# Context key and value projection moved beside the second norm, and the group steps laid out anew

## What is computed

```python
x = x + attn(layernorm(x))                        # causal, 16 heads of 32
h = ln(layernorm(x))                              # two norms in a row
q, k, v, qx = (round_fp8(h / s_i) * s_i @ w_i.T for each of the four)  # 8 groups, 2 heads of 128 each
kx, vx = split(ctx @ w_kv_x.T)                    # 8 groups of 128, no rounding
q, k, qx, kx = (ln of every head's 128 values)
core = softmax(q @ k.T / sqrt(128)) @ v           # 512 keys
xout = softmax(qx @ kx.T / sqrt(128)) @ vx        # 1024 keys
x = x + round_fp8(concat(core, xout) / smooth) @ wproj.T * scale
x = x + top-p mixture of 8 experts (layernorm(x))
```

## Time and profile before

| | |
|---|---|
| median of three runs | 2743.81 us (2742.49 to 2744.0) |
| the profiled execution: time, span | 2739.35 us, 2736.8 us |
| TensorE busy | 2386.2 us, 87% of the span |
| VectorE busy | 1414.3 us, 52% |
| ScalarE busy | 1133.5 us, 41% |
| GpSimd busy | 1044.1 us, 38% |
| first norm and causal attention | 0 to 306 us |
| second norm | 306 to 361 us |
| group attention: up to its first maximum | 361 to 407 us |
| its 16 steps, with the drain | 407 to about 1750 us |
| experts | to the end, TensorE full |

### The profile page before, as it was taken

How to read it: one execution, slowest core, us unless ns; L and a number is a source line. 1 busy time by engine, 2 the same in 40 slices (tenths; PEclk the granted TensorE clock), 3 DMA queues, 4 the chain that set the end, 5 groups by cost and what they waited for, 6 DMA issues and landing times. The chain is left out here.

```text
span 2736.8 us, 43666 instructions
## 1 busy us (share of the span) xinstructions
PE 2386.2 (87%) x15296; PEld 1424.9 (52%) x15296; DVE 1414.3 (52%) x3100; ACT 1133.5 (41%) x2101; POOL 1044.1 (38%) x1219
## 2 busy tenths in 40 slices
PE   6999457888888888788888876799999999999999
PEld 4666245566555566556566543344444444444444
DVE  5666747676676676667676666522222132322221
ACT  4555536565665555566566653211111112111110
POOL 3421235555564463635555341322131313122231
PEclk9898669899999999999999989799999999999999
DMA  3100005464554544555464454401011010112000
GB/s 130 45 21 1 1 1 110 81 120 90 98 107 81 100 99 91 109 97 93 83 116 92 83 103 83 185 32 62 31 61 61 31 61 31 61 34 88 0 0 31
DMA packets 414120, 191.69 MB, mean 70 GB/s; under 512 B 403568, under 2 KB 404080, under 8 KB 407280
## 3 DMA queue, kind: packets, MB, share of 16 engines
q1 hardware_dynamic: 410768, 166.29, 27.5%
q10 hardware_dynamic: 3168, 23.07, 2.6%
HBM read 86.56 MB, written 2.10 MB: 32 GB/s over the span
## 5 line engine op out<-in xcount | busy, mean ns | idle before, releaser
L1602 ACT ACTIVATE sil<-bank 128x512 f32<-128x512 f32 x128 | 76.4, 597 | 772.5 <-PE bank L289 772.5
L1293 DVE TENSOR_REDUCE xnm<-bank 128x1 f32<-128x512 f32 (+1 forms) x256 | 244.9, 957 | 263.7 <-PE bank L289 263.7
L1575 POOL TENSOR_SCALAR hh<-h 128x512 f16<-128x512 f32 x128 | 104.8, 819 | 680.7 <-DVE h L1673 680.7
L1673 DVE TENSOR_TENSOR h<-bank,sil 128x512 f32<-128x512 f32 x128 | 88.5, 692 | 530.7 <-PE bank L289 423.2
L1304 DVE SCALAR_TENSOR_TENSOR xparts<-xprob,xri,xparts 128x512 f16<-128x512 f32 (+1 forms) x256 | 271.2, 1060 | 105.5 <-ACT xparts L1210 103.7
L1210 ACT ACTIVATE xparts<-xprob,xri 128x512 f16<-128x512 f32 (+1 forms) x256 | 240.9, 941 | 204.6 <-DVE xri L1299 150.0
L1202 ACT ACTIVATE xprob<-bank,xnm 128x512 f32<-128x512 f32 (+1 forms) x256 | 231.3, 903 | 134.4 <-DVE xnm L1293 132.5
L287 PE MATMUL bank<-eXTh,ewh_gate 128*128 128x512 f16 x512 | 194.7, 380 | 3.5 <-DVE ewl_gate L1620 3.5
L288 PE MATMUL bank<-eXTh,ewl_gate 128*128 128x512 f16 x512 | 194.6, 380 | 0.0
L289 PE MATMUL bank<-eXTl,ewh_gate 128*128 128x512 f16 x512 | 194.6, 380 | 0.0
L287 PE MATMUL bank<-eXTh,ewh_up 128*128 128x512 f16 x512 | 194.1, 379 | 0.4 <-DVE ewl_up L1620 0.4
(11 more groups left out here) (247 smaller groups left out, 6242.1 us busy)
## 6 DMA issues: line engine op xcount, KB each, us to landing
xwraw<-in_w_group ACTq DMA_DIRECT2D x22, 1024.0 KB, 5.5
raw_gate<-in_gate SPq DMA_DIRECT2D x8, 2048.0 KB, 7.6
raw_up<-in_up SPq DMA_DIRECT2D x8, 2048.0 KB, 8.0
raw_down<-in_down SPq DMA_DIRECT2D x8, 2048.0 KB, 7.8
craw<-in_ctx SPq DMA_DIRECT2D x4, 1024.0 KB, 7.5
xpt<-xparts SPq DMA_TRANSPOSE x256, 4.3
wraw<-in_w_qkv SPq DMA_DIRECT2D x4, 768.0 KB, 4.4
X<-in_x SPq DMA_DIRECT2D x8, 256.0 KB, 5.0
```

The costliest lines, as they stand in the source:

```text
L1293: dve.tensor_reduce(nm[:, s:s + 1], SC[u % 2][:, 0:L], AX.X, ALU.max, negate=True).then_inc(maxed, 1)
L1575: pool.tensor_scalar(hh[half][:, f, :], h[i % 2][:], 1.0, 1.0, ALU.mult, ALU.mult).then_inc(h_hi, 1)
L1602: act.activation(sil[i % 2][:], bank[:, 2 * (i % 2), :], ACT.Silu, scale=1.0 / WS).then_inc(silu, 1)
L1673: dve.tensor_tensor(h[i % 2][:], bank[:, 2 * (i % 2) + 1, :], sil[i % 2][:], ALU.mult).then_inc(made, 1)
```

## The change

The projection of context keys and values leaves the group steps. `second_norm` now runs it for all groups: 4 pairs of groups by 2 batch entries by 8 context tiles, 64 tiles, each 12 matmuls of 512 columns into one of four PSUM banks, with the key norm (16 blocks at a time, the shifts half on GpSimd and half on VectorE), the key turns, and the high and low parts; the result goes to a DRAM tensor `kv_d`. The norm's own turns and roundings are placed between the tiles. The first pair's weights are split in the causal stage. Behind the phase all semaphores so far are cleared and freed, and a barrier follows. A group step loads keys and values of its batch entry from `kv_d` (a DMA of 1024 KB each, issued by ScalarE).

The steps are laid out anew: no C, T5 and T6 jobs; A and B one per unit in units 0 to 5, Y in 8 to 11, T in 12 to 15; product lag 6 instead of 4; 8 slots for turned parts instead of 4; 4 buffers for the parts instead of 2; q parts for both batch entries; GpSimd applies all 20 shifts; the weights of k and v in a chunk and a buffer of their own; the order of the instructions within a unit is another on VectorE and on ScalarE.

```diff
@@ -85,41 +85,54 @@
     out_d = out.rearrange("b (t p) d -> (b t) p d", p=P)
...
         with ExitStack() as ctx:
             rows2 = norm_rows(sem, lambda n, s, d: sbuf(ctx, n, s, d), "n2")
             rcols = sbuf(ctx, "rcols", [P, COLS], F32)
...
+            gw = [sbuf(ctx, f"x{x}", [P, KT, c], F16)
+                  for x, c in (("w1h", S), ("w1l", S), ("w2h", 2 * DH), ("w2l", 2 * DH))]
+            kv_d = nc.dram_tensor("kv_made", (B, GROUPS, P, KV), F16, kind="Internal").ap()
+            with ExitStack() as cross:
+                cxh, cxl = (sbuf(cross, x, [P, KT, B * SX], F16, "right") for x in ("cxh", "cxl"))
+                kvw = [[sbuf(cross, f"kv{x}{i}", [P, KT, S], F16, "right") for x in ("h", "l")] for i in range(2)]
+                kvraw = sbuf(cross, "kvraw", [P, KT, S], F32, "right")
+                with ExitStack() as c1:
+                    XTh = sbuf(c1, "XTh", [P, KT, T], F16)
...
                 with ExitStack() as c2:
-                    first_norm(nc, ins, sem, lambda n, s, d: sbuf(c2, n, s, d), bank, X, ident, cols, XTh, XTl, x_d, w)
-                with ExitStack() as c2:
-                    causal_attention(nc, ins, sem, lambda n, s, d: sbuf(c2, n, s, d), bank, X, ident, cols, XTh, XTl,
-                                     w, cxh, cxl, gw, rows2)
-            xq = sbuf(ctx, "xq", [P, 4, KT, T], F16)
+                    second_norm(nc, ins, sem, lambda n, s, d: sbuf(c2, n, s, d), bank, X, ident, cols, xq, rcols,
+                                rows2, cxh, cxl, kvw, kvraw, kv_d)
+            clear()
...
+                group_attention(nc, ins, sem, lambda n, s, d: sbuf(c2, n, s, d), bank, X, ident, cols, rcols, xq, kv_d,
+                                gw, rows3)
...
-    gwraw = [sb(f"gwraw{i}", [P, KT, S], F32) for i in range(2)]
+    gwraw = [sb("gwraw0", [P, KT, S], F32), sb("gwraw1", [P, KT, 2 * DH], F32)]
+    early = [(gwraw[0], gw[0], gw[1], group_scales(cols, 1)), (gwraw[1], gw[2], gw[3], group_scales(cols, 2)),
+             (kvraw, kvw[0][0], kvw[0][1], [(k, slice(0, S), WS) for k in range(KT)])]
...
 XT = SX // P
...
-SLOTS = 4
+SLOTS = 8
+PARTS_KEPT = 4
+LAG = 6
 P_SCALE = 2.0 ** 15
 PAIRS = UX // 2
-BLOCKS = KINDS * BT + BT + XT
...
+PAIRS_G = GROUPS // 2
+BATCH = XT
+BATCHES = PAIRS_G * B
...
+TURN_OFFSETS = (5, 6, 7, 7)
...
+def turns_at(i):
+
+    return [(i // BATCH - 1, r) for r, o in enumerate(TURN_OFFSETS) if i >= BATCH and i % BATCH == o]
...
+def norms_at(i):
...
+    j = i - NORM_FROM
+    return [j // NORM_EVERY] if j >= 0 and j % NORM_EVERY == 0 and j // NORM_EVERY < B * KT else []
...
+            for q in range(BATCHES):
+                gp, b = q // B, q % B
+                sp.wait_ge(c_low, BATCH * (q + 1))
+                for g in range(2):
+                    sp.dma_start(kv_d[b, 2 * gp + g, :, 2 * SX:4 * SX], vst[q % 2][:, g, :]).then_inc(v_stored[q % 2], 16)
+                if q in (0, 2):
+                    load(2 + q // 2)
+                for g in range(2):
+                    sp.wait_ge(t_lo, 4 * q + 2 * (g + 1))
+                    sp.dma_start(kv_d[b, 2 * gp + g, :, 0:2 * SX], kst[:, g, :]).then_inc(k_stored[g], 16)
...
+                for t in range(BATCH):
+                    a = kr[q % 2][:, 0, t, :]
+                    pool.tensor_scalar(a, a, rstd[:, t:t + 1], shift[:, t:t + 1], ALU.mult, ALU.add)\
+                        .then_inc(applied_pool, 1)
+                for r in range(4):
+                    k = 4 * q + r
+                    pool.wait_ge(t_read, k + 1)
+                    pool.tensor_tensor(key_part(r, 1), ft[k % 2][:], key_part(r, 0), ALU.subtract).then_inc(t_lo, 1)
+                if q in (1, 3):
+                    weights(2 + q // 2)
...
+                if i in (2, 3):
+                    normalise(1, i - 2)
+                if i == NORM_FROM:
+                    act.wait_ge(s_rcols, 2)
+                for j in norms_at(i - 1):
+                    scaled(j)
+                for q, r in turns_at(i):
+                    read_turned(q, r)
+            for r in range(4):
+                read_turned(BATCHES - 1, r)
...
         def _(dve):
+            def low(i):
+                q, t = i // BATCH, i % BATCH
+                dve.wait_ge(c_read, i + 1)
+                dve.scalar_tensor_tensor(out=value_part(i, 1), in0=cross_bank(i)[:, :, 1, :], scalar=1.0 / WS,
+                                         in1=value_part(i, 0), op0=ALU.mult, op1=ALU.subtract).then_inc(c_low, 1)
+                if q >= 2 and t == 0:
+                    dve.wait_ge(c_shift, q - 1)
+                for g in range(2):
+                    dve.bn_stats(stats[q % 2][:, BATCH * g + t, :], kr[q % 2][:, g, t, :]).then_inc(c_stats, 1)
...
+            for i in range(CROSS):
+                low(i)
+                for j in norms_at(i - 2):
+                    rounding(j)
+                if i >= BATCH and i % BATCH == 4:
+                    apply(i // BATCH - 1)
+                if i in (1, 27, 43):
+                    weights(1 + (1, 27, 43).index(i))
+            apply(BATCHES - 1)
...
+            def project(i):
+                gp, b, t = i // (B * BATCH), i // BATCH % B, i % BATCH
+                tok = slice(SX * b + P * t, SX * b + P * (t + 1))
+                wh, wl = kvw[gp % 2]
+                if i >= 4:
+                    pe.wait_ge(c_low, i - 3)
+                if i % (B * BATCH) == 0 and gp:
+                    pe.wait_ge(kw_lo, KT * gp)
+                for k in range(KT):
+                    ins_ = three(pe, bank[:, 2 + i % 4, :], cxh[:, k, tok], cxl[:, k, tok], wh[:, k, :], wl[:, k, :],
+                                 k == 0, k == KT - 1)
+                ins_.then_inc(c_done, 1)
...
-JOBS = "A0 A1 A2 A3 B0 B1 C0 C1 C2 C3 Y0 Y1 Y2 Y3 T0 T1 T4 T2 T3 T5 T6".split()
-
-SLOT_JOBS = {0: ("A0", "A1"), 1: ("A2", "A3"), 2: ("B0", "B1"), 3: ("C0",), 4: ("C1",), 5: ("C2",), 6: ("C3",),
-             7: ("Y0",), 8: ("Y1",), 9: ("Y2",), 10: ("Y3", "T0"), 11: ("T1", "T4"), 12: ("T2",), 13: ("T3", "T5"),
-             14: ("T6",)}
-APPLY_AT = {9: range(0, 5), 10: range(5, 11), 11: range(11, 4 * BT)}
-POOL_APPLIES = range(4 * BT, BLOCKS)
+            def turn(q, r):
+                k, g, half = 4 * q + r, r // 2, r % 2
+                if g == 0:
+                    pe.wait_ge(applied_pool, BATCH * q + BT * (half + 1))
+                else:
+                    pe.wait_ge(applied_dve, BATCH * q + BT * (half + 1))
+                if k >= 2:
+                    pe.wait_ge(t_read, k - 1)
...
+                ins_.then_inc(t_done, 1)
+
+            for i in range(CROSS):
+                project(i)
+                for j in norms_at(i):
+                    turn_norm(j)
...
+JOBS = "A0 A1 A2 A3 B0 B1 Y0 Y1 Y2 Y3 T4 T0 T1 T2 T3".split()
+
+SLOT_JOBS = {0: ("A0",), 1: ("A1",), 2: ("A2",), 3: ("A3",), 4: ("B0",), 5: ("B1",), 8: ("Y0",), 9: ("Y1",),
+             10: ("Y2",), 11: ("Y3",), 12: ("T4",), 13: ("T0",), 14: ("T1",), 15: ("T2", "T3")}
+APPLY_ORDER = [4 * BT + t for t in range(BT)] + list(range(4 * BT))
+OUTPUT_AT = {10: 0, 14: 1, 2: 2, 6: 3}
+ROUND_AT = {11: 0, 15: 1, 3: 2, 6: 3}
+QUANTISED_AT = {13: (0, 0), 0: (1, 1), 4: (2, 1), 7: (3, 1)}
 NEXT = [j for j in JOBS if j[0] != "Y"]
 T_ORDER = [j for j in JOBS if j[0] == "T"]
-V_ORDER = [j for j in JOBS if j[0] in "BC"]
+V_ORDER = [j for j in JOBS if j[0] == "B"]
 
...
-    return JOBS.index(name) % 2
+    i = JOBS.index(name)
+    return (i if i < 6 else i + 1) % 2
...
+                    if u in QUANTISED_AT and not (first and QUANTISED_AT[u][1]):
+                        kind, late = QUANTISED_AT[u]
+                        quantised(n - late, kind)
+                    if b == 0 and u == 4 and not last_group:
+                        split(1, 2 * g + 1, w_base(g), next_done, next_count("A3", n + 1), 4 * KT * g + 2 * KT)
+                    if b == 1 and u == 0 and not last_group:
+                        split(2, g + 1, w_base(g) + W1N, next_done, next_count("B1", n), 4 * KT * (g + 1))
                     if b == 1 and u == 3:
-                        split(3, 3 * g + 3 if not last_group else 3 * g + 1, w_base(g) + (0 if last_group else W1N + W2N),
+                        split(3, 2 * g + (2 if not last_group else 1), w_base(g) + (0 if last_group else W1N + W2N),
                               y_done, BT * (n - 1))
...
+            def load_kv(g, b, free):
+                wait(pved, free)
+                act.dma_start(kv[b][:], kv_d[b, bass.ds(g, 1)].rearrange("a p c -> p (a c)")).then_inc(kv_in[b], 16)
...
+                    exp(n, u)
...
-                    exp(n, u)
-                    if u in (0, 4) and not first:
-                        output(n - 1, 2 + u // 4)
...
-                    if u in (8, 12):
-                        if u == 8 and b == 0:
+                    if u in OUTPUT_AT and not (first and u < LAG + 2):
+                        if OUTPUT_AT[u] == 0 and b == 0:
                             act.wait_ge(s_rsm, g + 1)
```

(24 more changed lines are left out.)

407 lines of the change are left out of this document (231 added, 176 removed).

## The result

The changed kernel takes 2769.1 us (median of 7 runs, 2758.38 to 2769.47) against 2743.81: ratio 1.009, 95% interval 1.0067 to 1.0113. Forecast were 2727.8 us: the measured time lies inside the stated range (2676 to 2774), but on the other side of no change, so the sign was wrong. The profiled execution has a span of 2767.2 us. In the first lines of its page (busy us, share, instructions) VectorE and TensorE hardly differ from the table of before (1413.4 us against 1414.3, 2398.0 against 2386.2); GpSimd works 1138.1 us instead of 1044.1.

The account below looks back on a forecast made before the run. The prediction took the group steps to be bound by engines waiting for each other in a circle of PSUM banks, no engine full. Terms +160.9, -10, -6.5, -168.4, +7, +1 gave -16.0, hence 2727.8 us, range 2676 to 2774.

Parts of the forecast that it names:

- The phase: Second norm with the moved projection, to the barrier: 215.9 us against 55.0 before, so +160.9.
- both units' chains: Group steps: maximum, exponential, high part and low part follow one another, 4.77 us a long unit, 2.80 a short one.
- VectorE's phase: Rival: in the second norm GpSimd holds all VectorE's roundings, taken as +25 us, 2753 us in all; chance 0.11.
- the odd steps: Group steps with odd number: chains 60.6 plus units 0 to 5, unit 6, rounding and loop return, 71.5 us.
- The causal stage: Causal attention: four more weight parts on VectorE beside full TensorE, +1 us (0 to 3).
- Even steps: Group steps with even number: chains 60.6 plus small additions, 67.0 us each.
- behind a loop boundary VectorE's stall gives TensorE a start, +1.2: Units 0 to 5 of even steps: TensorE enters ahead, so they cost 1.2 us over the chain.
- unit 6: Group steps: output read behind the high part and rounded before the low part, +1.9 us; GpSimd's split in even steps, +2.7.
- The last step: Last group step: chain without the old overlap, plus one more product pair at the end, +7 us.
- the circle of banks: Old group steps: turning jobs wait for PSUM banks that VectorE empties a unit later, 108.4 us of TensorE's waits in 14 steps.
- Steps bound by TensorE: Rival: group steps are set by TensorE, not the chain, 66.7 us a step, 2682 us in all; chance 0.22.
- Slow clock: Rival: TensorE pauses and runs at 1.2 GHz from unit 8, 73.2 us a step, 2773 us in all; chance 0.17.

Follow-up runs that it names:

- e1: Changed kernel with the causal stage's low parts of the first group weights moved out of the units where GpSimd splits the context: 2758.54 us, ratio 1.0069.
- e3: Changed kernel with turning jobs one place earlier (T4 and T0 in unit 12, T1 in 13, T2 in 14, T3 in 15): 2739.77 us, ratio 0.9986.
- e13: Changed kernel with only the loop over groups 1 to 6 written out, so without a return: 2727.07 us, ratio 0.995.
- e2: Changed kernel with the order of instructions within a unit of the kernel before, on VectorE and ScalarE: 2653.2 us, ratio 0.9679.
- e5: Kernel before with one part of the change alone, the new order of instructions within a unit: 2757.61 us, ratio 1.0043.
- e8: Changed kernel with e1 and e2, and loads from DRAM moved (keys and values to unit 6, output weights to unit 15), lag 6: 2622.72 us, ratio 0.9547.
- e7: Changed kernel with e1 and e2, and lag 4 instead of 6, outputs read and rounded at earlier places: 2624.21 us, ratio 0.9542.
- e9: Changed kernel with the edits of e1, e2, e7 and e8 together (lag 4 and moved loads): 2619.29 us, ratio 0.9565.
- e4: Changed kernel with the rounding of the last output in unit 7 instead of unit 6: 2783.96 us, ratio 1.0158.
- e6: Changed kernel with the edits of e1, e2 and e3 together: 2656.02 us, ratio 0.9669.
- e11: e9 with 4 slots for transposed parts instead of 8 and 2 part buffers instead of 4: 2635.69 us, ratio 0.9618.
- e12: e9 with GpSimd's split of the next group's q weights cut into four pieces in units 12 to 15, and weight loads moved: 2682.37 us, ratio 0.9799.

## Why the prediction was wrong

**Right.** The phase (220.45 us against 215.9; from the last store's end at 536.8 to the barrier at 540.68 are the clearing's 3.9, forecast 3), the head (34.79 against 36.0), the first step (62.4 against 64), both units' chains (4.72 and 2.80 against 4.77 and 2.80). That VectorE's phase or a lower clock would decide did not happen: the clock of the 14 steps is 0.91 against 0.92. Right as a sum only, and in part by luck, are the odd steps (mean 72.6 against 71.5 + 0.75): units 0 to 5 cost 6.8 us over the chain instead of 5.0 (the rounding in unit 3, beside GpSimd's split, has no term); a return costs more than its 3.5, but there are five in the 14 steps and the sum has seven; and unit 8 takes 3.9 us, not the chain's 4.77. Not right is that T0 finds its bank empty: it still waits 2.1 us for X, which costs nothing behind the chain.

**The causal stage: +1 forecast, +14.3 measured.** The step "four more weight parts of 0.74 on VectorE beside full TensorE" counted the new instructions and not the new places of the old ones. The table of units moved low parts of the second chunk to where GpSimd splits the context. Holding was in the prediction, for the roundings only the earlier trace rows. Of the 14.3 us the maxima show 9.9 as holds, and e1 takes 8.0 of these away; 3.7 more are the stretch at half clock that lies elsewhere, which no run here explains.

**Even steps: 67.0 + 0.75 forecast, 71.2 measured; this is the step that failed.** Nearly all of the steps' 26.2 us lie here. The term "behind a loop boundary VectorE's stall gives TensorE a start, +1.2" supposes that VectorE is last at the return. TensorE is: the wait of T3 for the reading of T1 puts its last work late, the return takes it 4.15 to 5.02 us, and it enters the even step with no lead. Units 1 to 5 cost their full 3.70 and unit 0 5.5 us: 24.1 us for units 0 to 5, 7.3 over the chain, where the sum has 1.2 and 1.7 for half clock. e3 (TensorE earlier, 29 us less) and e13 (no return, 42 us less) show the return from two sides. In e13 units 0 to 5 of these steps still take 22.7 us, so the missing lead costs most of it, with or without a return. In the same way the return's term in odd steps, 3.46, measured 5.4 to 6.

A second term is mis-sized: the text prices unit 6 at +1.9, "and in the even steps (batch 0) GpSimd splits weights beside it, +2.7"; the sum of the even step has the 2.7 alone. Measured are 6.60 us, 3.8 over the chain's 2.80.

**The last step: +7 forecast, +12.2 measured to the end.** 6.05 us of it lie before the last maximum, the rest behind it. The forecast laid a part of this to one more product pair at the end. By the runs it is the order within a unit instead: e2, with the old order and lag 6, takes 46.85 us to its last maximum (before 53.50, changed kernel 59.55) and 1058.6 behind it (1057.4, 1063.6), while e5, with the new order and the old lag, takes 62.98 and 1063.0.

**What the forecast took as given.** The chain of 4.77 us was priced correctly and read as the cost of a step without the projection. It is the cost of the new order alone, and e2 shows 116 us for it. The price was right, so the sum has no error there; what the prediction lacks is the question whether those 4.77 us had to be. The trace of before answers it. Two maxima of VectorE there, in units of turning jobs:

```profile
1045.61 1.22 DVE L1293 TENSOR_REDUCE xnm<-bank 128x1 f32<-128x1024 f32 x1
...
1049.10 1.23 DVE L1293 TENSOR_REDUCE xnm<-bank 128x1 f32<-128x1024 f32 x1
```

3.49 us apart, in the old order: where the circle of banks left them alone, old units were quicker than the new chain.

**The rivals.** "Steps bound by TensorE" (0.22) came true only in units 1 to 5; with the old order also in units 9 and 10, and e2's step of 65.8 us is near the rival's 66.7, though TensorE is busy only 766.6 of 921.0 us there. "Slow clock" gave nearly the measured time (2773) by a mechanism that didn't occur.

The roundings in the steps were held, which the prediction had seen. VectorE in unit 6 of an even step, and GpSimd beside it:

```profile
1022.95 1.12 DVE L852 TENSOR_SCALAR xunit<-xy 128x512 uint16<-128x512 uint16 x1
1024.11 1.12 DVE L854 TENSOR_SCALAR xunit<-xunit 128x512 bf16<-128x512 bf16 x1
...
1020.50 4.59 POOL L1304 TENSOR_TENSOR xw1l<-xwraw,xw1h 128x512 f16<-128x512 f32 x4 [0.18 <-POOL xw1h L1301]
```

**Open.** Why the return costs TensorE up to 5.0 us in the changed kernel, 7.3 in e8 and nothing in e7. The record narrows it. Between e8 and e9 only the lag and the places of outputs and roundings differ, and e9 has no gap either; so it isn't the loads. The pages of the profiles add a difference that goes with it. In the changed kernel and in e7, the DMA queue q8 (packets, MB, share):

```profile
q8 instruction: 97, 1.59, 0.2%
```

```profile
q8 instruction: 52, 0.85, 0.1%
```

97 packets stand in the changed kernel, e1 to e4, e6 and e8, and 52 in e7, e9, e11 and e12, the kernels with a loop and lag 4: 45 fewer, nine for each of five returns. In e8 one such packet moves at 925 us and one at 929, inside or just ahead of the gap; at e7's return there is none. By these counts the gap stands where instructions are loaded again at each turn. That q8 is TensorE's queue, and why lag 4 spares it the loading, is not shown; nor is it the whole cause of a cost, since the kernel before has 100 packets and gaps of at most 1.4 us.

## What to carry to other kernels

The order of instructions within a step has no price of its own: the same order cost 13 us where a circle of banks set the pace and 116 us where that circle had been cut. After removing work, look up what the remaining cycle is made of, and try the other order first; here it turns 0.9% slower into 3.2% faster, and with the moved low parts, lag 4, moved loads and no loop into 4.7%. When a table of places changes, price every instruction that it moves by what the other engine does beside it, also the ones that aren't new.

## What the runs showed of the hardware

VectorE's low part (two inputs in SBUF, 128 columns, 0.3 us by itself) stood until GpSimd's instruction of 2048 columns had ended: 4.2 us beside one with two inputs, 2.04 beside one with a single input. A loop return cost VectorE 2.7 to 3.8 us and TensorE 4.15 to 7.3 us or nothing, about 8 us each in e13, in a body of some 145 us; gaps of that length came only in kernels whose page counts 97 instruction packets on q8, not in those with 52. Transposes and loads share the DMA engines: beside two loads of 1024 KB transposes took 13.9 us to land instead of 4.2 and made unit 12 2.7 to 5.6 us longer (e2 against e8); one load made it no longer.
